# One allocator for seven PSUM banks in a fused two-layer attention and expert kernel

## What is computed

```python
xn = layernorm(x)
x = x + cosformer(xn, Wq, bq, Wk, bk, Wv, bv, Wo, bo)      # 16 heads, linear attention
      + moe(xn, shared_up, shared_down, routed_up, routed_down, router_w)   # 16 routed experts, top 4, gelu
xn = layernorm(x)
x = x + rope_attention(xn, qw, kw, vw, ow)                 # 16 heads of 8, causal softmax
      + top1_experts(xn, router_w, router_b, w1, w2)       # 8 experts, 128 -> 2*512 -> 128, silu(a)*g, times max_prob
```

## Time and profile before

| | |
|---|---|
| time, median of 3 runs | 1339.46 us (1336.2 to 1342.16) |
| the profiled execution: its time | 1338.55 us |
| its span, first to last instruction | 1337.3 us |
| granted TensorE clock, mean | 0.969 |
| PE busy | 1209.6 us (90%) |
| DVE busy | 971.0 us (73%) |
| ACT busy | 919.6 us (69%) |
| POOL busy | 665.8 us (50%) |

### The profile page before, as it was taken

One profiled execution on the slowest core, in us unless ns is written; L12 is line 12 of the kernel. 1 busy time (PEld: TensorE's weight loads), 2 busy tenths in 40 slices (PEclk: granted clock), 3 DMA queues, 4 the chain that ended last, 5 costly groups with the idle time before them and its releaser, 6 DMA issues.

```text
span 1337.3 us, 28636 instructions
## 1 busy us (share of the span) xinstructions
PE 1209.6 (90%) x10216; PEld 702.9 (53%) x10216; DVE 971.0 (73%) x2442; ACT 919.6 (69%) x1233; POOL 665.8 (50%) x870
## 2 busy tenths in 40 slices
PE   2676999999999999999999999999997688989998
PEld 1342445454544545454545445454543257689998
DVE  2263888888888888898988888888877655345554
ACT  1141678777787868686878777787875557757776
POOL 6415364555545454636465554645464210138885
PEclk9788899999999999999999999999999689999999
DMA  7314426260606152442516060505155220024552
GB/s 230 64 42 83 96 30 116 56 127 18 116 21 114 32 101 63 72 90 45 103 31 131 11 125 21 113 22 113 42 92 166 74 82 22 15 36 61 61 61 27
DMA packets 90891, 97.77 MB, mean 73 GB/s; under 512 B 11008, under 2 KB 70528, under 8 KB 90368
## 3 DMA queue, kind: packets, MB, share of 16 engines
q1 hardware_dynamic: 78336, 86.96, 30.8%
q0 software_dynamic: 12416, 8.99, 5.3%
HBM read 69.09 MB, written 26.30 MB: 71 GB/s over the span
## 4 chain that ended last, share of the span: by engine, by line
PE 63%; DVE 18%; issue 5%; POOL 5%; ACT 5%; DMA 4%; SPq 0%; ACTq 0%; DVEq 0%; POOLq 0%
PE PS L629 10%; PE PS L596 8%; PE PS L441 7%; PE PS L485 6%; PE PS L562 4%; PE PS L640 4%; PE PS L581 4%; PE PS L424 4%; DMA early<-gate_rows 3%; DVE xn L831 3%; PE PS L435 2%; DVE nm L992 2%; PE PS L463 2%; PE PS L571 2%; POOL early L1139 1%
## 5 line engine op out<-in xcount | busy, mean ns | idle before, releaser
L1152 POOL TENSOR_SCALAR_AFFINE_SELECT flow<-flow 128x256 f32<-128x256 f32 (+1 forms) x448 | 190.3, 442 | 432.5 <-ACT flow L736 431.0
L736 ACT ACTIVATE flow<-PS 128x1024 f32<-128x1024 f32 x320 | 321.1, 1027 | 122.6 <-PE PS L581 105.3
L992 DVE TENSOR_REDUCE nm<-PS 128x2 f32<-128x1024 f32 x128 | 154.6, 1220 | 41.3 <-PE PS L550 37.7
L596 PE MATMUL PS<-flow 128*32 128x512 f32 (+3 forms) x2048 | 178.4, 449 | 5.4 <-POOL flow L1152 5.3
L1139 POOL TENSOR_TENSOR early<-early 128x512 f32<-128x512 f32 x128 | 160.4, 1267 | 18.1 <-DMA early<-gate_rows 17.1
L485 PE MATMUL PS<-early,down 128*128 128x512 f32 x288 | 151.9, 639 | 16.2 <-POOL early L1139 15.7
L727 ACT COPY qp<-PS 2x1024 f16<-2x1024 f16 x128 | 128.4, 1003 | 50.5 <-PE PS L571 49.4
L441 PE MATMUL PS<-xnT,up 128*128 128x512 f32 x288 | 153.4, 628 | 3.4 <-DVE at L915 3.4
L994 DVE TENSOR_REDUCE nm<-PS 128x2 f32<-128x768 f32 x128 | 121.6, 950 | 32.9 <-PE PS L550 32.8
L629 PE MATMUL PS<-xsT,w1s 128*128 128x128 f32 x1152 | 143.2, 278 | 2.1 <-DVE act L1091 2.1
L1176 POOL DMA_INDIRECT out_y<-X,rowu x72 | 112.2, 1559 | 62.0 <-ACT X L780 42.8
(11 more groups left out here) (170 smaller groups left out, 2194.3 us busy)
## 6 DMA issues: line engine op xcount, KB each, us to landing
early<-gate_rows SPq DMA_DIRECT2D x32, 1024.0 KB
qp<-relay_q SPq DMA_DIRECT2D x64, 128.0 KB
kp<-relay_k SPq DMA_DIRECT2D x64, 128.0 KB
xsb<-xs SPq DMA_DIRECT2D x72, 65.0 KB, 2.1
relay_k<-qkh SPq DMA_DIRECT2D x32, 128.0 KB, 2.3
out_y<-X SPq DMA_DIRECT2D x16, 256.0 KB, 2.9
early<-in_w SPq DMA_DIRECT2D x1, 4096.0 KB, 17.6
relay_q<-qkh SPq DMA_DIRECT2D x16, 128.0 KB, 2.3
```

The source lines that it names most:

```text
L596: ins = pe.matmul(m.PS[32 * j:32 * j + 32, m.PV, kt * P:], m.vst[b % 2][:, kt, 4 * g + j, :], m.pt[:, r, k * L + o:k * L + o + L - kt * P] ...
L736: act.activation(m.pt[:, n % RING, :], m.PS[:, i:i + 2, :].rearrange("p k c -> p (k c)"), ACT.Exp, scale=1.0 / SCALE).then_inc(s["exp"], 1)
L992: dve.tensor_reduce(nm[:, 3, 2 * n:2 * n + 2], ps, AX_X, ALU.max, negate=True).then_inc(s["max"], 1)
L1152: ins = pool.affine_select(part, part, [[0, part.shape[1]], [1, P]], ALU.is_ge, nothing, base=0, channel_multiplier=-1)
```

## The change

Seven banks (all but 4) are given out by one rule until the first expert tile. Each bank has an age, the turn at which it was last given out (for the bank of the `down` sum, its last stage). A pair stage takes, of (0, 1), (2, 3) and (5, 6), the pair whose younger bank is oldest. A single stage takes the oldest bank; a bank whose pair is still whole, that is, was last used as a pair, counts as 3 turns younger. From the first tile on, single stages have bank 7 and pairs are (0, 1) and (2, 3), as before. Since the two banks of a pair can now have been freed by different stages, `score_banks` waits once for each bank, and `hidden` of tile 0 and of tile 22 does too.

```diff
+PAIRS = ((0, 1), (2, 3), (5, 6))
+SPLIT = 3
+PAIRED = (0, NBETWEEN + NBETWEEN % 2)
...
-    turns, free, held = [5, 6, 7], [None] * 8, None
-    work, snext = {}, 0
+    turns, free, held = [], [None] * 8, None
+    work, age, whole, pairs = {}, [0] * 8, [True] * 8, list(PAIRS)
+
+    def touch(at):
+        age[at] = max(age) + 1
 
     def take():
-        at = turns.pop(0)
-        if at == held:
-            turns.append(at)
-            at = turns.pop(0)
-        turns.append(at)
+        if turns:
+            return turns[0]
+        at = min((at for at in (0, 1, 2, 3, 5, 6, 7) if at != held),
+                 key=lambda at: age[at] + (SPLIT if at < 7 and whole[at] else 0))
+        for one in PAIRS:
+            if at in one:
+                whole[one[0]] = whole[one[1]] = False
+        touch(at)
         return at
+
+    def take_pair():
+        got = min((one for one in pairs if held not in one), key=lambda one: max(age[one[0]], age[one[1]]))
+        for at in got:
+            touch(at)
+            whole[at] = True
+        return got
...
         if name in ("max", "score"):
-            work[stage] = [(snext, free[snext])]
-            free[snext] = ("max", b * G * NU + i + 1) if name == "max" else ("exp", b * NS + i + 1)
-            free[snext + 1] = free[snext]
-            snext = (snext + 2) % 4
+            got = take_pair()
+            work[stage] = [(at, free[at]) for at in got]
+            for at in got:
+                free[at] = ("max", b * G * NU + i + 1) if name == "max" else ("exp", b * NS + i + 1)
...
         if name == "down" and i == NC - 1:
-            free[held], held = ("yT", b + 1), None
+            free[held] = "yT", b + 1
+            touch(held)
+            held = None
...
             if i == 0:
-                turns = [7]
+                turns, pairs = [7], [(0, 1), (2, 3)]
...
         if name == "hidden":
             at = 5 if i < NBETWEEN or i % 2 else 0
-            work[stage] = [(at, free[at])]
+            work[stage] = [(at, free[at]), (at + 1, free[at + 1])]
...
     def score_banks(stage):
-        i, freed = work[stage][0]
-        if freed:
-            pe.wait_ge(s[freed[0]], freed[1])
+        for _, freed in work[stage]:
+            if freed:
+                pe.wait_ge(s[freed[0]], freed[1])
+        i = work[stage][0][0]
         return m.PS[:, i:i + 2, :]
...
-        bank(("hidden", 0, n))
+        for k in range(2 if n in PAIRED else 1):
+            bank(("hidden", 0, n), k)
```

## The result

After the change the kernel takes 1362.38 us, median of 4 runs (1359.45 to 1365.32), against 1340.2 us (1336.2 to 1342.16) before: ratio 1.0168, 95% interval 1.0145 to 1.0192. It is 1.7% slower; 1359 us, 1.5%, was forecast.

What follows compares the result with a forecast made beforehand. PE was taken to bound the kernel, busy 1209.6 of 1337.3 us. Middle 20.8, start 1.0 + 0.75, end -3, doubled waits 0.8 sum to 20.35 us on 1338.55: 1358.9, stated as 1359; 8-in-10 range 1344 to 1373.

Steps and rivals of the forecast that it cites:

- The second score of a batch: Batches 3 to 15: score 1 must wait for DVE's eviction of attn0, which took two single banks; 1.20 us, 13 times.
- xnT0: The next batch's xnT0 takes bank 7 from the down sum and waits for ACT's eviction: 0.25 us, 13 times.
- The doubled waits: Max and score stages wait once per bank: 0.25 us a batch, 0.8 us extra for the whole kernel, 16 us kept for range.
- the third rival: Every back-to-back pair stage pays 0.06 us for its second wait: 1374 us, chance 0.14.
- What is taken away in the middle: Score 5's bank wait of 0.2 us goes, the next max takes back half: 0.1 us gained a batch.
- The other middle waits unchanged: Sign to look for after the change: PE's middle waits, apart from the new ones at score 1 and xnT0, stay.
- Can the batch absorb it?: At mrows 3, the 1.06 us wait behind DVE moves along with PE's 1.6 us delay, so nothing is absorbed.
- The second rival: DVE catches up before mrows, whose waits shrink by 1.06 + 0.3 us a batch: 1341 us, chance 0.10.
- The start: kvr 1 waits for bank 7, 0.75 us; batch 2's scores and small items 1.0; up 2's dropped waits give nothing.
- The end: In the last batches the third pair removes pair waits before a nearly full DVE: 3 us gained, at most 14.6.
- the first rival: The third pair pays in full: all 14.6 us at the end go and PE keeps full clock; 1340 us, chance 0.08.

Runs made afterwards that it cites:

- experiment 1: The kernel before, where score 1 additionally waits for attn0's eviction of batch b + 2, nothing else changed: 1354.0 us, ratio 1.0114.
- `b_late`: The kernel before, with norm0 moved in DVE's order to behind the row-maxima tile that mrows 3 waits for: 1333.56 us, ratio 0.9948.
- `b_double_wait`: The kernel before, where each pair stage waits twice for the same semaphore and value: 1368.79 us, ratio 1.0233.
- `x_one_pair`: The kernel after, but attn0 takes one whole pair, gT takes bank 7 and v keeps off bank 7: 1372.59 us, ratio 1.0267.
- `x_pair_late`: The kernel after, with attn0 in one pair, gT in bank 7, v off 7, one wait per shared semaphore, norm0 behind the tile: 1335.61 us, ratio 0.9965.
- `x_one_wait`: The kernel after, where a pair whose banks wait for one semaphore waits once, for the later value: 1359.23 us, ratio 1.0139.
- `b_double_late`: The kernel before, with all pair stages waiting twice for the same value and norm0 behind the tile: 1336.3 us, ratio 0.9982.

## Why the prediction was right, step by step

**The second score of a batch** was the right mechanism at the right size: 1.20 us forecast, 0.12 + 1.11 = 1.23 measured (the eviction ends 1.08 us behind score 1's old place, and the release takes 0.15 where 0.11 was forecast), 14 waits of L602 as forecast (13.9 us over the whole run), and 15 us by itself in experiment 1.

**xnT0**: 0.25 forecast, 0.28 measured, 15 waits of 3.3 us in all.

**The doubled waits**: 0.25 us a batch forecast; 0.08 measured by taking them out of the kernel after, 0.17 by adding them to `b_late`, where they cost 2.7 us in all. The bound of 16 us was far too wide, and the third rival (1374) is out. The 1369 us of `b_double_wait` lies near that rival's figure, but by another mechanism.

**What is taken away in the middle**: 0.21 us at score 5, of which nearly nothing came back; and q's wait of the earlier trace rows, which the prediction held to stay, fell from 0.16 to 0.09 us. "The other middle waits unchanged" was wrong by small items: -0.07 at q, -0.16 at attn0, which gT, behind DVE's gate (L922), hands back (gT starts 7.82 us after q before, 7.83 after), +0.1 at the values behind POOL, +0.2 at max behind exp. Together: 1.58 us a batch against 1.60.

**Can the batch absorb it?** No, as forecast: 1.06 us at mrows 3 before and after, and nearly the same, 1.57 us, with that wait at 0.62. The second rival (1341) is out. The prediction's reason was half of the truth: DVE's run to mrows 3 starts when PE feeds it, but its length is set by POOL, and the prediction did not see this. In the kernel after the phase happens to be the good one; in `x_one_pair` it was not, and by that the same reasoning would have been wrong by some 30 us.

**The start** was mis-sized: 0.75 + 1.0 = 1.75 us forecast, 4.0 measured at batch 3. kvr 1 came 0.81 us late (27.78 against 26.98), about as worked out:

```profile
27.78 2.65 PE L455 MATMUL PS<-wkv,xnT 128*128 128x273 f32 x5 [0.54 <-DVE early L877]
```

But a saved wait did not cost nothing downstream. In batch 1 attn0 starts 1.2 us earlier and runs for 3.55 us in place of 2.20; the windows 90:94 before and 89:94 after show the clock under it:

```profile
90.00:94.00 4.00, 2.80 (x20) 2.29 (x20) 3.47 (x23) 1.80 (x3) 0.49 (x1) 1.00 0.23 64
```

```profile
89.00:94.00 5.00, 4.49 (x21) 4.04 (x22) 3.47 (x23) 0.61 (x3) 0.41 (x1) 0.66 0.17 48
```

and the first gated product lets go of PE later:

```profile
111.95 2.07 PE L505 MATMUL PS<-early,down 128*128 128x512 f32 x2 [9.92 <-POOL early L1161]
```

against an idle time of 6.62 us until 110.00 before. The stretch was written off as hidden behind the gates' transfer; the transfer itself moved. The traces tell how far: SyncE issues it only 0.27 us later (96.03 against 95.76 us), while POOL's first product behind it starts 1.95 us later (110.63 against 108.68). So the way from the issue to the product is 1.7 us longer, and what PE lost at the lower clock ahead of the issue accounts for 0.3 us at most. Why the transfer took longer stays open: no run changed the start alone. Nor is the 4.0 us shown to belong to the change: of the kernels whose norm0 is not ahead, attn0 of batch 3 starts at 208.0 to 210.1 us in the five with the old banks and at 209.5 to 214.1 in the five with three pairs, `x_pair_late` being the earliest of these with the same late kvr 1.

**The end**: 3 us forecast, 3.3 measured between the two profiled executions. One such pair would not show it, for the stretch from score 1 of batch 13 to the end scatters: it takes 374.5 to 380.3 us in the seven kernels with the old banks and 370.8 to 377.8 in the seven with three pairs. Their means, 377.5 and 374.1, differ by 3.4, with a standard error of 1.2. Waits of PE over the same stages, before (985 to 1077 us) and after (1009 to 1098 us), the largest rows of each:

```profile
PE PS L562 <- DVE nm L995: 5.2, 4, 3.1
PE PS L571 <- DVE mt L1011: 5.0, 3, 2.7
PE PS L562 <- ACT flow L736: 3.1, 4, 0.8
PE PS L581 <- ACT flow L736: 1.9, 5, 0.7
```

```profile
PE PS L592 <- DVE mt L1033: 6.6, 3, 5.1
PE PS L602 <- DVE nm L1017: 1.9, 2, 1.2
PE PS L592 <- ACT xsT L786: 1.7, 1, 1.7
PE PS L583 <- DVE nm L1017: 1.5, 3, 0.7
```

The pair stages' waits fell by about half, and much of it came back at mrows: batch 14's 19th maximum is 2.91 us less late than the stage before it, and its mrows 3 then loses 2.40. In the tables' stretch DVE is busy 21.30 of 24 us where it was 19.67 in the earlier trace rows, at a clock of 0.51 where it was 0.52:

```profile
1059.00:1083.00 24.00, 15.48 (x126) 6.57 (x126) 21.30 (x44) 10.85 (x12) 5.12 (x9) 0.51 0.37 114
```

A deeper queue ahead of a nearly full engine gave back some of that engine's idle time, and the first rival (1340) is out: neither the 14.6 us nor the clock came.

The sum was closer than its parts, and that is luck: the start was 2.25 us too low, the middle with the doubled waits (21.6 forecast, 20.0 measured) 1.6 too high, the end 0.3 too small a gain.

## What to carry to other kernels

When several buffers are pooled, look at the stage that takes two at once: if it takes one out of each of two pairs, it spoils both, and the next pair stage that finds no whole pair waits for its eviction (here 1.23 us a batch). Before trusting a sum of small shifts, look for instructions on the critical path whose length depends on what another engine does beside them; a shift of 0.1 us can cost more than 1 us there, and a kernel tuned by hand may stand on a lucky phase. A test of one cause should be run in two phases of such a place (here norm0 in the old place and behind the tile), or it measures the phase.

## What the runs showed of the hardware

- A TENSOR_SCALAR of DVE on SBUF data, 128x128 float32, takes 0.33 us alone and up to 2.9 us beside POOL's TENSOR_TENSOR; the tile's TENSOR_TENSOR 1.18 in place of 0.23 us. In the rows that were looked at singly, each long one ends 0.08 to 0.14 us behind a POOL product. The Trainium skill, SBUF — State Buffer, "Who interferes with whom", says that VectorE and GpSimd share one pair of ports, and that the one that issues first holds it for the whole instruction while the other fully blocks. That norm0 takes 5.59, 3.06 to 4.19 or 1.10 us by its place agrees with such a lock; no run took POOL's products away to show it directly. The order does not come out of the records: a DVE instruction that starts 0.67 or 0.82 us before the product's record, with only an AFFINE_SELECT of POOL in between, is held to the product's end as well, and why is open.
- A second wait of PE on a semaphore already raised costs 0.08 (`x_one_wait` against after) to 0.17 us a batch (`b_double_late` against `b_late`), with 40 such pair stages in one.
- After a wait of 2.3 us PE's granted clock fell to a mean of 0.57 over 4 us in one batch of `b_double_wait` (window above) and stayed at 1.00 in another, 131 us earlier, after an equal wait.
